# A block and its router over four periods instead of three, attention as q times k, and the residual added in PSUM

## The reference, cut to what matters

```
def attn_ref(q_x, ...):                     # q_x = layernorm(x), first norm
    xn = ln(q_x, ln1_w, ln1_b)
    q, k, v = (xn @ w + b split into 16 heads of 16)
    fq, fk = elu(q) + 1, elu(k) + 1
    kv    = einsum('bhnd,bhne->bnde', fk, v)        # sum over the heads h of one token
    qkv   = einsum('bhnd,bnde->bhne', fq, kv)
    qk    = einsum('bhnd,bnd->bhn', fq, fk.sum(axis=1))
    x     = q_x + (qkv / (qk[..., None] + 1e-06)) @ wo + bo
    h     = gelu(ln(x, ln2_w, ln2_b) @ fc_w + fc_b)           # 256 -> 1024
    return x + (h @ proj_w + proj_b)
def ffn_ref(x, ...):                        # x = layernorm(x), third norm
    logits = x @ gate_w.T                   # 8 experts, top 2, softmax over the two
    out    = sum of w_e * (silu(x @ wg[e].T) * (x @ wu[e].T)) @ w_down[e].T    # 256 -> 384 -> 256
    shared = silu(x @ sg_gate.T) * (x @ sg_up.T) @ sg_down.T
    return shared + out
x = x + attn_ref(layernorm(x), ...)
return x + ffn_ref(layernorm(x), ...)
```

## Time and profile before

| | us |
|---|---|
| median of three runs (lowest, highest) | 1912.48 (1909.49, 1914.32) |
| profiled execution, its time | 1909.86 |
| its span, mean granted TensorE clock | 1908.1, 0.935 |
| PE busy in the span | 1739.2 (91%) |
| DVE busy | 1275.3 (67%) |
| POOL busy | 1270.5 (67%) |
| ACT busy | 772.7 (40%) |

### The profile page before, as it was taken

The page is one execution under the profiler, slowest core; times in us unless marked ns, Lnnn a source line. Parts: engine busy times, 40 slices in busy tenths (PEclk is TensorE's granted clock), DMA queues, the critical chain, the costliest instruction groups (busy, mean ns, idle before and its releaser), DMA issues.

```text
span 1908.1 us, 25917 instructions
## 1 busy us (share of the span) xinstructions
PE 1739.2 (91%) x7160; PEld 1247.1 (65%) x7161; DVE 1275.3 (67%) x2291; ACT 772.7 (40%) x1518; POOL 1270.5 (67%) x749
## 2 busy tenths in 40 slices
PE   3489998999999999998999899797999999999997
PEld 1255665555656655665566566555888888888886
DVE  7999898988988989889889899613222222222221
ACT  2245455354454453544544534431333322333222
POOL 4877888888888888889888888802333333333333
PEclk8699898898998988989989889888999999999999
DMA  5001110110101101101011010106777777677674
GB/s 188 27 29 44 45 45 23 44 38 28 44 11 44 44 22 44 42 25 44 15 41 44 22 44 34 41 4 187 157 162 163 162 158 157 161 163 164 158 155 90
DMA packets 87130, 148.57 MB, mean 78 GB/s; under 512 B 8640, under 2 KB 71872, under 8 KB 86720
## 3 DMA queue, kind: packets, MB, share of 16 engines
q1 hardware_dynamic: 60512, 112.58, 18.9%
q0 software_dynamic: 26592, 35.67, 11.2%
HBM read 101.79 MB, written 48.56 MB: 79 GB/s over the span
## 4 chain that ended last, share of the span: by engine, by line
PE 47%; POOL 26%; DVE 14%; issue 8%; ACT 3%; DMA 1%; POOLq 0%; DVEq 0%; SPq 0%; ACTq 0%
POOL prod_pool L464 10%; PE p_b L1362 10%; PE p_b L1373 10%; PE p_q L1362 7%; PE p_b L1301 6%; DVE prod L838 4%; POOL prod_pool L537 3%; PE p_v L1362 3%; POOL prod_pool L482 3%; PE p_b L1222 3%; POOL rows_sorted L501 3%; POOL prod_pool L520 3%; DVE prod L863 2%; PE p_b L1270 2%; DVE kvT L846 2%
## 5 line engine op out<-in xcount | busy, mean ns | idle before, releaser
L577 POOL DMA_INDIRECT out_rows<-prod_pool,prod x142 | 220.9, 1555 | 384.3 <-ACT prod_pool L756 353.8
L464 POOL TENSOR_TENSOR prod_pool<-prod_pool 128x544 f32<-128x544 f32 (+4 forms) x240 | 400.0, 1667 | 18.8
L1270 PE MATMUL p_b<-bT,fc_sb 128*128 128x512 f32 x512 | 225.6, 599 | 12.1 <-ACT bT L683 12.1
L1222 PE MATMUL p_b<-proj_sb,hid 128*128 128x256 f32 x1024 | 230.5, 379 | 0.0
L846 DVE TENSOR_REDUCE kvT<-prod 128x128 f32<-128x2048 f32 x96 | 219.5, 2286 | 2.7
L838 DVE TENSOR_TENSOR prod<-p_q,v_dve 128x4096 f32<-128x4096 f32 x48 | 211.9, 4415 | 0.0
L1222 PEld LDWEIGHTS p_b<-proj_sb,hid 128*128 128x128 f32 x1024 | 189.6, 190 | 27.7 <-issue 0.5
L1301 PE MATMUL p_b<-bT,sgup_sb 128*128 128x512 f32 x384 | 206.5, 695 | 0.0
L1362 PE MATMUL p_b<-prod,exp_up 128*128 128x256 f32 x840 | 187.1, 379 | 0.0
L1270 PEld LDWEIGHTS p_b<-bT,fc_sb 128*128 128x128 f32 x512 | 96.5, 191 | 131.8 <-issue 108.1
L876 DVE TENSOR_REDUCE qkv<-prod 128x204 f32<-128x3264 f32 x48 | 170.4, 3550 | 4.0 <-DVE rs_a L808 3.2
(11 more groups left out here) (164 smaller groups left out, 2867.0 us busy)
## 6 DMA issues: line engine op xcount, KB each, us to landing
exp_up<-in_experts SPq DMA_DIRECT2D x71, 768.0 KB, 4.7
prod<-rows_sorted SPq DMA_DIRECT2D x71, 260.0 KB, 2.8
xin<-in_x SPq DMA_DIRECT2D x16, 512.0 KB, 3.4
xres<-in_x SPq DMA_DIRECT2D x16, 512.0 KB, 3.6
out_rows<-x SPq DMA_DIRECT2D x16, 512.0 KB, 3.3
exp_dn<-in_experts SPq DMA_DIRECT2D x8, 384.0 KB, 5.5
out_rows<-prod_pool,prod POOLq DMA_INDIRECT x142, 3.8
rows_sorted<-rows SPq DMA_DIRECT2D x2, 1040.0 KB, 6.7
```

What stands on the lines that cost most here:

```text
L464: done(g.tensor_tensor(prod_pool[:, at:at + n * w], prod_pool[:, at:at + n * w], prod_pool[:, at + n * w:at + 2 * n * w], ALU.add))
L577: pool.indirect_dma_start(out=out[:, :], out_offset=bass.IndirectOffsetOnAxis(ap=tok_i[j][:, a:a + 1], axis=0), in_=yg[j][:, a * D:(a + 1) ...
L1222: ins = t_.matmul(o, src[:, k, t * P:(t + 1) * P], w[:, k, :], start=k == 0, stop=bias_at is None and k == chunks - 1)
L1270: ins = t_.matmul(bnk[:], fc_sb[:, k, f * P:(f + 1) * P], bT[:, k, :], start=k == 0, stop=k == KC - 1)
```

## The change

1. **Attention by q times k.** For each token the 16 x 16 scores fq·fk are made first (4096 products, summed over 16), then the scores times v (4096 products, summed over the 16 key heads). The divisor is the sum of a row of scores, so that the column of ones is gone. The key weights stand head by head now. Unit 2 alone is shared: 8 heads on DVE, 8 on POOL (`heads(c)`, once a period); unit 0 is POOL's, units 1 and 3 DVE's. Some small operands move to PSUM (`gap_1`, `first2`, the first value of `rows`' expert).
2. **Residual in PSUM.** `to_tokens(..., plus=xmid)` adds xmid by a product with the identity inside proj's accumulation; POOL's L534 and its semaphore go, and `residual_2` adds xres.
3. **Four periods.** `stage_b` of block c-1 ends with residual_2 and the third norm's variance; ACT takes ln and exp of it at the end of its body (`scales_3`). `stage_c` of block c-2: `shift_3` on DVE behind its first product, normed rows, their transposes on PE behind wo, the projection of unit 2, the logits, then `choose`; ranks inside fc behind chunk 5 (`RANKS_AT`), place, weights, scatter; `shared_up` behind proj. `stage_d` of block c-3: down product, finish, store. `x1` and `rows` are doubled, so that the loop holds two periods (`periods`); `sg_g`, `sg_u` and the transposed rows `x3T` have their own space; logits and ranks lie in the second half of the p_xT bank.

The diff, cut:

```diff
-DVE_HEADS = 12
-POOL_HEADS = HEADS - DVE_HEADS
+SPLIT = 2
+POOL_HEADS = 8
+RANKS_AT = 5
 ORDER = (POOL_TILE, 0, 1, 2)
-POOL_STEPS, DVE_STEPS = 21, 74
-HE = HD + 1
+POOL_STEPS, DVE_STEPS = 16, 79
+HH = HEADS * HD
...
+            for c in range(FIRST):
+                body(c, c)
+            with eng.Fori(0, PAIRS) as m:
+                if chain:
+                    chain.enter(m, steps)
+                body(2 * m + FIRST, 0)
+                body(2 * m + FIRST + 1, 1)
+                if chain:
+                    chain.leave(PAIRS)
...
+            def scores(q, k, n):
+
+                return g.tensor_tensor(
+                    prod_pool[:, 0:n * HH].rearrange("p (d h g) -> p d h g", d=HD, g=HEADS),
+                    q.rearrange("p (h d) -> p d h", d=HD).unsqueeze(3).to_broadcast([P, HD, n, HEADS]),
+                    k.unsqueeze(2).to_broadcast([P, HD, n, HEADS]), ALU.mult)
+
+            def mixed(sc, v, n):
+
+                return g.tensor_tensor(
+                    prod_pool[:, 0:n * HH].rearrange("p (g h e) -> p g h e", g=HEADS, e=HD),
+                    sc.rearrange("p h g -> p g h").unsqueeze(3).to_broadcast([P, HEADS, n, HD]),
+                    v.unsqueeze(2).to_broadcast([P, HEADS, n, HD]), ALU.mult)
...
+                    wait(pool, attn_ready, c)
+                    done(halve(flat(s_pool[:, 0:HEADS, :])))
+                    announce(pool, mixed(s_pool[:, 0:HEADS, :], v_pool[:], HEADS), pool_v_used, c + 1)
+                    done(halve(flat(qkv_pool[:, 0:HEADS, :])))
+                    heads(c)
+                if stage_c:
+                    scatter(c, j)
...
+            def scales_3(c):
+
+                wait(act, x1_read, c)
+                a.activation(sq_c[:], mv_c[:, :, 1], ACT.Ln, bias=eps_1[:, 0:1]).then_inc(ln3_log, 1)
+                act.wait_ge(ln3_log, c)
+                wait(act, rows_ready, TPB * (c - 1))
+                a.activation(rs_c[:, 0, :], sq_c[:], ACT.Exp, scale=-0.5).then_inc(ln3_std, 1)
...
+                wait(act, ln3_scale, c - 1)
+                if isinstance(c, int) and c == 2:
+                    act.wait_ge(init_stored, 48)
+                wait(act, scattered, 16 * 2 * TPB * (c - 3))
+                norm(lambda t: rows[j % 2][:, t, 0:D], lambda t: x1[j % 2][:, t, :], rs_c, rows_ready)
...
+            def products_1(u):
+                done.sync()
+                n = own_heads(u)
                 done.later(v.tensor_tensor(
-                    prod[:, 0:HD * HD * HEADS].rearrange("p (e d h) -> p e d h", e=HD, d=HD),
-                    fk.unsqueeze(1).to_broadcast([P, HD, HD, HEADS]),
-                    v_dve[u % 2][:].unsqueeze(2).to_broadcast([P, HD, HD, HEADS]), ALU.mult))
-
...
+            def products_2(c, u, free):
                 done.sync()
-                n = DVE_HEADS
+                n = own_heads(u)
                 ins = v.tensor_tensor(
-                    prod[:, 0:n * HE * HD].rearrange("p (h e d) -> p h e d", h=n, e=HE),
-                    p_qk[u % 2][:, 0:n * HD].rearrange("p (h d) -> p h d", h=n).unsqueeze(2)
-                    .to_broadcast([P, n, HE, HD]),
-                    kvT[u % 2][:].unsqueeze(1).to_broadcast([P, n, HE, HD]), ALU.mult)
+                    prod[:, 0:n * HH].rearrange("p (h e g) -> p h e g", h=n, e=HD),
+                    p_qk[u % 2][:, 0:n * HEADS].rearrange("p (h g) -> p h g", h=n).unsqueeze(2)
+                    .to_broadcast([P, n, HD, HEADS]),
+                    v_dve[u % 2][:].unsqueeze(1).to_broadcast([P, n, HD, HEADS]), ALU.mult)
...
+            def residual_2(c, j, k):
+
+                x1_b = x1[(j + 1) % 2]
+                if k == 0:
+                    wait(dve, xres_loaded, 16 * c)
+                    wait(dve, out_stored, 16 * (c - 2))
+                    wait(dve, rows_ready, TPB * (c - 2))
+                flat, res = (z[:].rearrange("p t d -> p (t d)") for z in (x1_b, xres))
+                wait(dve, proj_psum, 2 * (c - 1) + k + 1)
+                done(v.tensor_tensor(flat[:, 512 * k:512 * k + 512],
+                                     res[:, 512 * k:512 * k + 512], (p_b0, p_b1)[k][:], ALU.add))
+                for t in range(TPB // 2 * k, TPB // 2 * (k + 1)):
+                    done.later(v.bn_stats(st6[:, t, :], x1_b[:, t, :]))
+                if k == 1:
+                    averages(mv_b)
+                    v.tensor_copy(mv_c[:], mv_b).then_inc(x1_read, 1)
+
+            def shift_3(c):
+
+                wait(dve, ln3_std, c - 1)
+                done(v.scalar_tensor_tensor(shift_c, mv_c[:, :, 0], -1.0, rs_c[:, 0, :], ALU.mult, ALU.mult))
+                v.tensor_copy(rs_c[:, 1, :], shift_c).then_inc(ln3_scale, 1)
+
...
-                    kv_products(1)
-                    kv_sums_1(1)
+                    products_1(1)
+                if stage_c:
+                    shift_3(c)
+                if core:
+                    sums_1(1, 0, half)
                 if stage_b:
                     residual_1(c)
                 if core:
                     keep_scales(c)
+                    if more:
+                        ln1_stats(c + 1)
                 if stage_b:
...
                                         stop=bias_at is None and k == chunks - 1)
+                    if plus is not None:
+                        t_.matmul(o, ident[:], plus[:, t, :], start=False, stop=False)
                     if bias_at is not None:
...
                               at_last_chunk=lambda: wait(pe, attnT_ready, KC * c))
+                if stage_c:
+                    transpose_block(rows[j % 2], (p_b0, p_b1), x3T_psum,
+                                    lambda t: wait(pe, rows_ready, TPB * (c - 2) + t + 1))
                 if core:
                     project_x(c, 2, "P")
-                if tail:
-                    wait(pe, shared_h, c - 1)
-                    if not stage_b:
-                        wait(pe, ranks_read, c - 1)
-                    to_tokens(sg_g, HCH, sgdn_sb, (p_b0, p_b1), None, down_psum)
+                if stage_c:
+                    logits(c)
+                if stage_d:
+                    down(c)
                 if stage_b:
                     transpose_block(hnorm, (p_b2, p_b3), hT_psum,
                                     lambda t: wait(pe, h_ready, TPB * (c - 1) + t + 1))
-                if core and not stage_b:
-                    project_x(c, 3, "P")
-                if stage_b:
...
+                    ranks(c)
+                if core:
+                    project_x(c, 3, "P")
+                if stage_b:
...
+                    if stage_c and more:
+                        wait(pe, ranks_read, c - 1)
                     to_tokens(hid, FCH, proj_sb, (p_b0, p_b1), 4 * D, proj_psum,
                               at_last_chunk=lambda: wait(pe, gelu_ready, FCH * c),
                               between=(lambda u: project_x(c + 1, u, "T")) if more else None,
-                              per_bank=True)
+                              per_bank=True, plus=xmid)
                 elif more:
                     project_x(c + 1, 0, "T")
                     project_x(c + 1, 1, "T")
...
+            def shared_up(c):
+
+                for n in range(2 * HCH):
+                    if n >= 2:
+                        wait(pe, up_taken, 2 * HCH * (c - 2) + n - 1)
```

653 lines of the change are left out of this document (324 added, 329 removed).

## The result

| | before | after |
|---|---|---|
| median of four runs (lowest, highest) | 1911.20 (1909.49, 1914.32) | 1878.33 (1877.24, 1879.65) |
| profiled execution, span | 1909.86, 1908.1 | 1879.65, 1877.6 |
| mean granted TensorE clock | 0.935 | 0.968 |

The ratio is 0.9826, with a 95% interval of 0.9809 to 0.9843: the change makes the kernel 1.7% faster, 33 us. The forecast was 1858 in a range of 1826 to 1898. The direction and the range held; the time is 20 us above the forecast, and of the forecast gain of 54 us 33 came.

A forecast was written before the change was run, and what follows sets the result against it. Bound before: a two-period loop through POOL, DVE, ACT and PE; after: PE's loop. Fifteen periods -58.9, first block -6.7, drain +12.5 give -53.1 from 1909.9: 1856.8, plus 2.6 for the timed median, forecast 1858; range 1826 to 1898.

The forecast's parts named there:

- The hold: DVE's shift_3, with two SBUF inputs, waits for POOL's 4.5 us addition to end: 1.9 us a period; without it 1832, chance 0.24.
- the nearest row (L948): A DVE cast in the kernel before, all operands in SBUF, ending with POOL's additions; taken as model for shift_3's added wait.
- The period: One block's turn in the loop: PE's 70.9 us plus 1.9 of wait at shift_3, 72.8, say 72.7.
- so the 3.13 + 0.96 us of standing go, and with them, I take it, the low clock: At the router, PE no longer stands and TensorE's reduced clock, costing 4.7 us a period, goes too.
- the second rival: TensorE's clock stays low in part of each period: 1.5 to 3.5 us a period, 1879 to 1907, or 1924; chance 0.20.
- clock 0.5 after the row transposes: Sign in the profile after, on PE at the router, that the forecast is wrong.
- none was to be over 2.3: Sign of being right: PE stands only before wo, rows and fc, never longer than 2.3 us.
- The drain: After the last attention: 6.3 us more to proj's end, 11.7 to the rows, 5.5 less to the slots; +12.5 in all.
- Ends of the pipeline: First attention 6.7 us earlier; period 1 takes 66.5, period 2 69.9, period 15 68.2 us.
- The rival that POOL becomes the bound: Unit 0's product elements on POOL cost 2.45 ns, not 1.845: POOL needs 74.0 us a period, total 1880; chance 0.08.

The follow-up runs named there:

- e3: Changed kernel with 16 transposes of the identity added on PE directly ahead of the row transposes; 1868.76 us, ratio 0.9781 to the kernel before.
- e1: Changed kernel with shift_3's mean first copied to PSUM, so its product has one SBUF input; 1847.40 us, ratio 0.9674 to the kernel before.
- e10: Changed kernel with shift_3's mean copied to PSUM, and the logits moved ahead of unit 2's projection; 1908.91 us, ratio 0.9981 to the kernel before.
- e6: Changed kernel with the residual sum back on POOL and PE's four identity products removed; 1853.06 us, ratio 0.9693 to the kernel before.
- e9: Changed kernel with 3.55 us more DVE work a period, an unread sum over 3264 products; 1901.89 us, ratio 0.9942 to the kernel before.

## Why the prediction was right in its mechanism and 20 us short

**The hold** was sized at 1.9 us a period and is 1.92 on the mean. It was the disputed term, and the nearest row (L948) was the right model. The size came from the right places too: shift_3 comes 5.1 to 5.2 us into DVE's period (forecast 5.2), and POOL's addition starts at 1.8 to 3.1 (2.6), for single holds of 1.2 to 2.4.

**The period** was to be 72.7. Five of twelve are 72.4 to 72.9, the seven others 74.1 to 74.6. The step that failed is "so the 3.13 + 0.96 us of standing go, and with them, I take it, the low clock". The stand of 3.13 came back as one of 2.0 to 2.6, made by the hold, and in seven of twelve periods the clock falls for 3 to 4 us behind it. That is the second rival's place and its price (1.5 to 3.5 a period; measured 74.3 - 72.6 = 1.7), in little over half of the periods: the rivals were weighed as alternatives, and what came was the forecast with half of one. One of the prediction's own signs of being wrong, clock 0.5 after the row transposes, came in those seven, and PE's longest stand was 2.59 us where none was to be over 2.3. 12 x (73.7 - 72.7) = 12 us. e3, with the stand filled, makes the kernel 9.6 us faster.

**The drain** was to cost 12.5 and costs 105.55 - 87.2 = 18.4. Up to proj's end 8.5 for the forecast 6.3, because PE stands 3.39 us for the last attention and wo and the down product run at low clock; from there to the rows 11.0 for 11.7, right; from the rows to the slots -1.3 for -5.5. There "the low clock's share goes" failed once more: behind PE's stand of 2.60 us the transposes, the logits (3.55 us) and the down product all run at the low clock. A projection does not stand between there, but that alone does not decide it: the logits at 1184.02 us have none either and took 1.92. In all the drain missed 6 us.

**Ends of the pipeline.** The first attention comes 6.4 earlier (6.7 forecast). Period 1 takes 67.9 for 66.5, period 2 70.3 for 69.9, period 15 71.2 for 68.2: 4.8 us more.

12 + 6 + 4.8 = 23 is what the sum missed; the profiled execution took 1879.65 for its 1856.8.

**DVE and POOL** were right: products and sums by element count, POOL's own period 73.7 - 4.8 = 68.9 for 69.0. (The 17.8 us of a full tile are 17.6 by their own terms; 17.7 were measured.) The rival that POOL becomes the bound is out. **PE's** work is 819.2 / 12 = 68.3 us at full clock (e1) for 67.6.

What the prediction did not ask is which part earns the gain. e10, e6 and e9 say: the place of the projection is worth 61 us, the time saved on DVE 24, and the residual in PSUM costs 25. They were not all measured on the same kernel (e10 on e1), so they do not add up to 33. What POOL's new share of the attention and the later scatter are worth was not tested.
